# A state-space scan in tiles of four states by thirty-two channels, run on from one sequence into the next

## The reference, cut to what matters

```python
x = x + _layernorm(_L1_attn_ref(_layernorm(x), ...))     # the Mamba layer, third of four blocks
...
delta = jax.nn.softplus(dt_full + b_dt)                  # 512 channels by 512 tokens
def step(state, inp):                                    # over the 512 tokens
    u, dlt, Bs, Cs = inp
    dA = jnp.exp(dlt.reshape(b, NC, DPG)[..., None] * A_g)
    du = (dlt * u).reshape(b, NC, DPG)
    state = dA * state + du[..., None] * Bs[:, :, None, :]
    y = jnp.einsum('bgdn,bgn->bgd', state, Cs).reshape(b, D_INNER)
    return (state, y)
...
y = (ys.transpose(1, 0, 2) + x.transpose(0, 2, 1) * D_param) * jax.nn.silu(z)
return y @ W_out.T
```

## Time and profile before

| what | value |
|---|---|
| median of 3 runs | 2097.48 us |
| the profiled execution's own time | 2099.33 us |
| its span, first to last instruction | 2097.5 us |
| mean granted TensorE clock | 0.899 |
| VectorE (DVE) busy | 1770.0 us, 84% |
| TensorE matmuls (PE) busy | 1651.5 us, 79% |
| ScalarE (ACT) busy | 1035.9 us, 49% |
| GpSimd (POOL) busy | 913.8 us, 44% |
| DMA, share of 16 engines | 23%, 157.95 MB |
| the eight scans, first to last | 231.47 to 2001.45 us |

### The profile page before, as it was taken

One profiled execution on the slowest core, in us unless ns is written; L12 is line 12 of the kernel. 1 busy time (PEld: TensorE's weight loads), 2 busy tenths in 40 slices (PEclk: granted clock), 3 DMA queues, 4 the chain that ended last, 5 costly groups with the idle time before them and its releaser, 6 DMA issues. The chain is left out here.

```text
span 2097.5 us, 22567 instructions
## 1 busy us (share of the span) xinstructions
PE 1651.5 (79%) x5875; PEld 725.3 (35%) x5948; DVE 1770.0 (84%) x3142; ACT 1035.9 (49%) x1745; POOL 913.8 (44%) x676
## 2 busy tenths in 40 slices
PE   3375577778996889868997799878997899779856
PEld 1122123232452335322452335332452335234324
DVE  6577899989879998979989998999989987987830
ACT  3247444825555454735556355734547344734312
POOL 0101534454437434554346434464346544665510
PEclk9977699979997999979997899979997899999978
DMA  4100222222222222222231222222222223223300
GB/s 108 46 0 21 72 79 89 92 69 77 75 92 65 85 71 86 85 67 78 74 101 65 81 76 76 96 75 72 76 96 71 76 85 106 86 99 113 110 10 11
DMA packets 94601, 157.95 MB, mean 75 GB/s; under 512 B 10940, under 2 KB 23660, under 8 KB 94468
## 3 DMA queue, kind: packets, MB, share of 16 engines
q1 hardware_dynamic: 94468, 156.43, 22.9%
HBM read 143.83 MB, written 12.58 MB: 75 GB/s over the span
## 5 line engine op out<-in xcount | busy, mean ns | idle before, releaser
L1226 POOL TENSOR_TENSOR prod<-state,c_all 128x512 f32<-128x512 f32 x512 | 669.6, 1312 | 706.8 <-DVE state L1203 644.0
L1203 DVE TENSOR_TENSOR_SCAN state<-decay,ps_b 128x512 f32<-128x512 f32 x512 | 619.7, 1210 | 9.7 <-issue 0.4
L750 PE MATMUL ps_y<-prod,idf 128*128 128x512 f32 x1024 | 610.6, 689 | 4.8 <-DVE u L1216 3.6
L1210 DVE TENSOR_TENSOR ps_b<-du,ps_b 128x512 f32<-128x512 f32 x512 | 347.7, 679 | 87.3 <-PE ps_b L743 86.8
L919 ACT ACTIVATE decay<-delta,a_neg 128x512 f32<-128x512 f32 x512 | 359.3, 719 | 32.3 <-DVE state L1203 29.3
L743 PE MATMUL ps_b<-b_rows,sel_b 48*128 48x512 bf16 x512 | 209.9, 411 | 155.0 <-DVE state L1203 152.7
L750 PEld LDWEIGHTS ps_y<-prod,idf 128*128 128x128 f32 x1024 | 183.8, 207 | 136.3 <-issue 109.9
L743 PEld LDWEIGHTS ps_b<-b_rows,sel_b 48*128 48x128 bf16 x512 | 47.8, 94 | 467.3 <-DVE state L1203 332.5
L619 PE MATMUL ps_x<-xT,w 128*128 128x512 bf16 (+1 forms) x391 | 132.0, 422 | 80.1 <-DVE arena_l L1095 65.6
L826 ACT ACTIVATE arena_l<-ps_x 128x512 f32<-128x512 f32 (+1 forms) x104 | 61.8, 594 | 190.8 <-PE ps_x L619 189.7
L535 PE MATMUL ps_x<-hT,win 128*128 128x512 bf16 (+1 forms) x455 | 135.6, 441 | 21.4 <-DVE arena_b L1171 16.6
(11 more groups left out here) (230 smaller groups left out, 2422.2 us busy)
## 6 DMA issues: line engine op xcount, KB each, us to landing
c_all<-c_rows SPq DMA_DIRECT2D x512, 256.0 KB
c_rows<-arena_l SPq DMA_DIRECT2D x32, 256.0 KB
out<-arena_b SPq DMA_DIRECT2D x8, 512.0 KB
x_in<-in_base SPq DMA_DIRECT2D x8, 256.0 KB
c_all<-in_winT SPq DMA_DIRECT2D x1, 1280.0 KB, 7.5
arena_b<-in_w_fc SPq DMA_DIRECT2D x1, 1024.0 KB, 5.7
arena_b<-in_w_proj SPq DMA_DIRECT2D x1, 1024.0 KB, 5.0
w<-in_w1T SPq DMA_DIRECT2D x1, 792.0 KB, 5.9
```

Source lines behind the costliest of these rows:

```text
L750: nc.tensor.matmul(ps_y[:], idf[:], prod[:, n % NP, :], start=(n % NST == 0), stop=(n % NST == NST - 1)).then_inc(reduced, 1)
L1203: nc.vector.tensor_tensor_scan(state[:, n % NS, :], decay[:, n % NDA, :], ps_b[:, n % NDB, :], 0.0, ALU.mult, ALU.add).then_inc(scanned, 1)
L1210: nc.vector.tensor_tensor(ps_b[:, j % NDB, :], du[:, slot(s, ct), :], ps_b[:, j % NDB, :], ALU.mult).then_inc(driven, 1)
L1226: nc.gpsimd.tensor_tensor(prod[:, n % NP, :], state[:, n % NS, :], c_all[:, n % NC, :], ALU.mult).then_inc(multiplied, 1)
```

## The change

A tile now has 32 channels with four states each: partition 64g + 16s + c holds channel 16g + c of the 32 and state s of the four. A block of 128 channels still has 16 tiles: n % 4 (called q) says which 32 channels, n % 16 // 4 which four states.

- **Sums.** The selector `sel_y` (128x32) adds the four states of each channel and puts out 32 columns, into partitions 32q to 32q+31 of `ps_y`. The sums of tiles 4m to 4m+3 stand together in part 2 of step 4m+6, behind one wait for all four, with one semaphore update behind the last. So `ps_y` takes four matmuls of 32 columns in place of four of 128, the number of matmuls is the same, and GpSimd's wait for tile n-4 to be summed becomes one for the group.
- **delta and du** are no longer usable as they are computed. `d_store` (two DMAs of 256 KB a block) puts them into DRAM, and `scan_sync` reads them back repeated (for each q, two DMAs of 128 KB for delta and two for du) in the steps 12 to 15 of a block, once the tile in this place is decayed and driven: 16 DMAs a block, 64 a sequence, and 8 stores. SyncE's 64 loads of C stay.
- **Run on.** `tile_at` maps a tile outside 0 to 63 to the neighbouring sequence. The steps are 0 to 63 only; the last tiles of s are scanned, multiplied and summed in the first steps of the iteration of s+1, without empty steps between. LATE is laid into the steps 0 to 60, BACK and GATE into the steps 6 to 63. Within a slot the chains come ahead of the scan.
- The logarithm of softplus now comes after `d_fix`, the storage of its steps is moved, and exp(A_log) is laid out and negated on ScalarE.

```diff
         def scan_pe(...):
+                nc.tensor.matmul(ps_b[:, n % NDB, :], sel_s[lo:lo + 48, part_n, :],
                                  b_rows[lo:lo + 48, s.par, ct // 2, :], start=True, stop=True).then_inc(b_spread, 1)
-            if part == 2:
-                for n in sums_at(j):
-                    if n % NST == 0:
-                        wait(eng, y_taken, s.count(PER, n))
-                    eng.wait_ge(multiplied, s.count(PER, n + 1))
-                    nc.tensor.matmul(ps_y[:], idf[:], prod[:, n % NP, :], start=(n % NST == 0),
-                                     stop=(n % NST == NST - 1)).then_inc(reduced, 1)
+            s, n = tile_at(at, j - 3)
+            if part == 2 and exists(s) and n % QN == QN - 1:
+                ct, part_n, q = parts(n)
+                if part_n == 0:
+                    wait(eng, y_taken, s.count(PER, NST * ct))
+                eng.wait_ge(multiplied, s.count(PER, n + 1))
+                for q in range(QN):
+                    ins = nc.tensor.matmul(ps_y[q * QC:(q + 1) * QC, :], sel_y[:], prod[:, (n - QN + 1 + q) % NP, :],
+                                           start=(part_n == 0), stop=(part_n == QN - 1))
+                ins.then_inc(reduced, QN)
...
         def scan_sync(...):
+            for n in range(-QN, 0) if j == -1 else [j] if j % NST >= NST - QN else []:
+                q = n % QN
+                s, to = tile_at(at, n + QN)
...
+                eng.wait_ge(d_stored[ct], stored)
+                wait(eng, decayed, used)
+                wait(eng, driven, used)
+                for kind, rep in enumerate((delta, du)):
+                    rows = d_rows[s.par, ct, kind].rearrange("(q g o c) t -> q g o c t", q=QN, g=QG, o=1)[q]
+                    for g in range(QG):
+                        eng.dma_start(rep[64 * g:64 * (g + 1), q, :],
+                                      rows[g].broadcast_to([QN, NST, T])).then_inc(d_spread[q], 16)
...
-        SLOTS = [(j, part, 1.0 if 0 <= j <= PER else 0.25) for j in STEPS for part in range(3)]
+        SLOTS = [(j, part) for j in range(PER) for part in range(3)]
+        ALL = [1.0] * len(SLOTS)
+        AHEAD = [1.0 if j < PER - 3 else 0.05 for j, _ in SLOTS]
+        BEHIND = [1.0 if j > Y_LAG else 0.0 for j, _ in SLOTS]
...
-            for k, (j, part, _) in enumerate(SLOTS):
-                fns["scan"](eng, s, j, part)
+            for k, (j, part) in enumerate(SLOTS):
                 for slots in chains:
                     run_steps(e, eng, fns, slots[k])
+                fns["scan"](eng, s, j, part)
```

More of the change, by code:

```diff
@@ L29 @@
 NST = 16
+QN = 4
+QC = P // QN
+QG = QC // NST
 NXB = 4
@@ L335, in sandwich @@
         u = sb("u", [P, 2, CT, T])
-        delta, du = (sb(n, [P, CT + 1, T]) for n in ("delta", "du"))
+        delta, du = (sb(n, [P, QN, T]) for n in ("delta", "du"))
+        d_r = sb("d_r", [P, 2, T])
         NC, NDA, NDB, NS, NP = 5, 4, 2, 3, 4
@@ L436, in sandwich @@
         out_stored = sem("out_stored")
+        d_stored = [sem(f"d_stored{i}") for i in range(CT)]
+        d_spread = [sem(f"d_spread{i}") for i in range(QN)]
         b_spread = sem("b_spread")
@@ L822, in late_act @@
                     wait(eng, late["V"], s.count(LPER, 0))
+                    for k in range(CT):
+                        wait(eng, d_stored[k], s.count(PER, 0))
                 if i >= 2:
@@ L861, in late_act @@
                 eng.wait_ge(late["P"], la(s, "P", ("d", i)))
-                free_slot(eng, s, i)
+                for k in range(2):
+                    if i == 0:
+                        wait(eng, d_stored[k], s.count(PER, 0))
+                    elif i == 2:
+                        eng.wait_ge(c_stored[k], s.count(PER, PER))
                 bank = D_BANK[i]
                 act(d_t(i), ps_x[:, bank, :], ACT.Abs, bias=b2[:, i:i + 1])
-                ins = act(delta[:, slot(s, i), :], ps_x[:, bank, :], ACT.Relu, bias=b2[:, i:i + 1])
+                ins = act(d_raw(i), ps_x[:, bank, :], ACT.Relu, bias=b2[:, i:i + 1])
             elif name == "d_exp":
@@ L1453, in program @@
             together(e, eng, fns, tagged("late", Seq(0), LATE), tagged("early", Seq(1), EARLY), tagged("quant", None, QUANT))
+            for part in range(3):
+                fns["scan"](eng, Seq(0), -1, part)
             iteration(e, eng, fns, Seq(0), first=True)
@@ L1459, in program @@
                 iteration(e, eng, fns, Seq(n))
+            for j in range(PER, PER + Y_LAG):
+                for part in range(3):
+                    fns["scan"](eng, Seq(NBATCH - 1), j, part)
             alone(e, eng, fns, tagged("back", Seq(NBATCH - 1), BACK))
```

203 lines of the change are left out of this document (119 added, 84 removed).

## The result

The changed kernel takes **2591.8 us** (median; the undisturbed runs are 2588.9 to 2593.3, and one of 4202 us is left out as disturbed), the kernel before 2096.4 in the same series: ratio 1.235, 95% interval 1.230 to 1.239. It is 495 us slower, where 2049 us, 2% faster, was forecast. The span is 2591.5 us and the mean granted clock 0.721, against 0.899.

What follows compares the result with a forecast made beforehand. VectorE, 91% full, was taken to set the time. Start 235.5, sequences 219, 1144, 195.6 and 156.8, tail 97.5: 2048.6 us; 2050.4 with 1.8 around the span, less 1.9 for the median: 2049 us, range 1988 to 2115.

Steps and rivals of the forecast that it cites:

- Spreading delta and du, "at nothing": SyncE's stores and repeats at changes of block: issues fit the steps and landings are hidden, so no added time.
- The forecast's slack: Repeats on SyncE: the one for tile n is due four steps, 14 us, after its issue can start.
- The rival of late repeats: SyncE's in-order queue: repeats wait behind loads of C, 1.5 us at each of 31 block changes, 2096 us; chance 0.10.
- theory C: From the experiments, not the prediction: SyncE's order puts repeats behind loads of C; no size at the start.
- The added wait, 3 us a sequence: GpSimd's four product buffers return together, so product and scan wait: 3 us a sequence, 22 in the last.
- S + 2.0 against a room of 5.55: Middle sequences: from scan 4m+5's end, the group's time plus 2.0 us must fit VectorE's 5.55 us of other work.
- The wait for the spread of B, 10.3 becomes 6: VectorE's drive waiting for TensorE's spread: falls with TensorE's load, from 10.3 to 6 us a middle sequence.
- S, 2.5 us: Time of a group of four sums on TensorE: staggered halves in five places, 2.15 us, plus 0.33 for switches.
- side by side in full: Rival for TensorE's four sums: all run at once, a group takes 0.9 to 1.2 us, 1997 us total; chance 0.22.
- the emptying at a switch of shape: TensorE switching to 32 columns and back: at most about 0.17 us each, 0.33 for two.
- The lower clock: Rival for a lighter TensorE: half speed for a third of groups, some 40 us, 2090; within the forecast's range, no separate chance.
- VectorE's busy time: Sign in the profile after: VectorE still busy 217 us a sequence, its instructions unchanged.

Runs made afterwards that it cites:

- e1: The changed kernel with each repeat reading 64 consecutive rows instead of 16 rows four times, giving wrong delta and du: 2311.6 us, ratio 1.103.
- e5: The changed kernel with channels outermost and copies inside, a repeat being one 128-row transfer and a load of C two of 64 rows: 2281.7 us, ratio 1.091.
- e11: e5 with the sums issued in pairs of column groups instead of fours: 2102.8 us, ratio 1.003.
- e13: e5, still with groups of four sums, with six product buffers instead of four and two decay buffers instead of four: 2138.7 us, ratio 1.021.
- e7: e5 with every spread of B issued three times, adding 1024 short matmuls without changing results: 2373.8 us, ratio 1.133.
- e10: The kernel before the change, with only the dealing of both chains over the steps taken from the change: 2173.7 us, ratio 1.037.

## Why the prediction was wrong

**The two causes.** They form a square: fours and copies outermost 2592 (the change), fours and channels outermost 2282, pairs and copies outermost 2429, pairs and channels outermost 2103. The layout is worth 310 with fours and 326 with pairs, the pairs 163 and 179. They add up nearly, and together, 489 us, they are nearly all of the 495. What is left after both, some 6 us, is a balance: the new dealing (77 on the kernel before) and the repeats (16) against what the run-on and the sums side by side win. That balance was not taken apart further, and how much of it is the run-on stays open.

**Spreading delta and du, "at nothing": the step that failed first.** It took the landing time of 128 KB, 2.7 us, from a load of the weights with 128 partitions outermost, for a transfer whose outermost size is 4. The four tiles' repeats move 2 MB; at the 100 GB/s of the trace they need some 20 us by themselves, and with the loads of C on the same engines the tiles came 7 us apart: from the first issue at 931.9 to the fourth tile's decay at 962.6 are 31 us. The forecast's slack was 14 us for the first tile and three steps of 3.4 more for the fourth, 24 in all. The number of issues was right, their length not: 0.51 us alone, but up to 2.98 us while much is queued:

```profile
L1354 SPq DMA_DIRECT2D delta<-d_rows x256: 507/525/2977, 225.5 to 2447.1; - x128
```

The rival of late repeats named the place (the change of block) and priced it at 1.5 us; 310 / 31 is 10. It looked at SyncE's queue, which is theory C, and with all engines at work the repeats as a whole cost 16 us.

**The added wait, 3 us a sequence: the second.** The formula, S + 2.0 against a room of 5.55, was right about who waits for whom, and its S was even too large. What failed is the sentence behind it, "TensorE's own chain work stands ahead of some groups: I put 3 us". In the middle sequences 71 of 80 groups made GpSimd wait, and two things come between a product and its sum. One is the steps' chain matmuls, up to 5.7 us in one piece in e1. The other is TensorE's own wait: the group stands behind a spread of B, and the spread waits for a scan. Spreads did so 116 times in these sequences, for 251 us of idle TensorE, though not all of them ahead of a group. Around the group at 1055.48 this is 6.5 of the 13.7 us that GpSimd stood:

```profile
1054.95 0.60 PE L770 MATMUL ps_b<-b_rows,sel_s 48*128 48x512 bf16 x1 [6.49 <-DVE state L1236]
...
1057.67 1.26 POOL L1260 TENSOR_TENSOR prod<-state,c_all 128x512 f32<-128x512 f32 x1 [13.68 <-PE ps_y L779]
```

Late repeats add to the second, by the scans that they hold up: with channels outermost (e5) GpSimd's wait for the sums is 919 us of 1140. The kernel before hid all this: a buffer came back after each sum, and GpSimd had three more. 179 us over the run, some 22 a sequence, against the 3 (22 in the last) of the forecast. How it divides between the two was not measured.

**The wait for the spread of B, 10.3 becomes 6.** Wrong in its direction: it is 109.5 us in the five middle sequences, 22 each. The sum held that a TensorE with less to do would be less late; in e1's rows the same 5.7 us of chain matmuls hold up the spread.

**S, 2.5 us.** Wrong, and the rival "side by side in full" right: 1.06 us at the high clock. In the changed kernel at the low one:

```profile
1055.48 1.93 PE L779 MATMUL ps_y<-prod,sel_y 128*32 128x512 f32 x8
```

Eight halves in 1.93 us at 1.2 GHz, where the earlier trace rows has four halves in 3.79. The second half of a sum does stand behind its first, as I argued, but the first halves of the other sums do not wait for it. TensorE in e1, in 772.2 to 772.4 and in 772.75 to 773.0:

```profile
772.06 0.64 PE L779 MATMUL ps_y<-prod,sel_y 128*32 128x512 f32 x4
...
772.51 0.61 PE L779 MATMUL ps_y<-prod,sel_y 128*32 128x512 f32 x4
```

The four first halves start within 0.02 us, the four second halves 0.45 us behind them: two places, not five. The other term of S, the emptying at a switch of shape, can be read off too. The next matmul of 128x128 starts 0.43 us behind the start of a sum's last half in the kernel before, and 0.52 behind it in e1 (the fourth of the halves below starts at 847.69). The first two rows are of the kernel before, in 1223.2 to 1223.6, the others of e1, in 848.05 to 848.5:

```profile
1222.92 0.59 PE L750 MATMUL ps_y<-prod,idf 128*128 128x512 f32 x1
1223.35 0.59 PE L722 MATMUL ps_x<-arena_b,fcT 128*128 128x512 f32 x1
...
847.67 0.61 PE L779 MATMUL ps_y<-prod,sel_y 128*32 128x512 f32 x4
848.21 0.70 PE L749 MATMUL ps_x<-arena_b,fcT 128*128 128x512 f32 x1
```

That is 0.1 us a switch at the high clock, where I allowed 0.17. The Trainium skill, "TensorEngine Tiling (Array Packing)", Key Properties, names such an emptying; the trace agrees in that a pause stands there, with this time. But toward a spread of B, 48 rows by 128 columns, the kernel before has it already: 0.53 us from 1961.55, the last half of the sum at 1961.12 in the earlier trace rows, to the spread at 1962.08. That TensorE had less to do did help where single sums became pairs; with groups of four the order took it back, and the rival's 1997 us fails with the forecast's wait.

**The lower clock.** It came, 0.72 for 0.91 in the middle sequences, lower than that rival had it, but nothing here shows it as a large cause of its own: e11 runs at 0.81 and takes what the kernel before takes, e13 takes 143 us less than e5 at the same clock, and more matmuls did not raise it (e7). It lengthens the chain matmuls that stand ahead of a group, which is part of the 179; how much was not separated.

**What held.** VectorE's busy time; the end of the wait for `ps_y` at the ends of a sequence; the tail (97.5 forecast, 96.2); a new wait of the scan for GpSimd, but in all sequences. The gap between the last scan of a sequence and the first of the next did not close: from start to start 5.5 to 7.7 us in six places and 16.8 in one (8.0 to 15.7 before); with channels outermost and pairs (e11) five of the seven are 2.6 to 2.9 us, so there the gap is closed as forecast. The first scan was to come at 235.5 and came at 241.98. The repeats for tiles 0 to 3 and the loads of C behind them were slow there as well:

```profile
225.48 1.44 SPq L1354 DMA_DIRECT2D delta<-d_rows  x2
...
234.57 0.72 ACT L942 ACTIVATE decay<-delta,a_neg 128x512 f32<-128x512 f32 x1 [6.76 <-DMA du<-d_rows]
...
241.98 1.19 DVE L1236 TENSOR_TENSOR_SCAN state<-decay,ps_b 128x512 f32<-128x512 f32 x1
```

**The arithmetic.** The terms of the sum add up to 2048.4 and not 2048.6, and 16 instructions of 256 columns in 3.72 us give 0.44 and not 0.43 us for 512; neither matters.

**What was not in it:** the dealing of the chains. In e10 the sum of the steps' weights falls from 66 to some 61.5 for one chain and 59.8 for the other, which looked like nothing, and costs 77 us.

## What to carry to other kernels

Before a transfer is put down as hidden, price it by a row of its own shape, with the outermost dimension above all: copies outermost cost 310 us more than channels outermost here, and with channels outermost the same bytes cost 16. When work is grouped, count the buffers that come back together against the longest stretch of other work ahead of the group on its engine, not against the group's own time; half the group in the same buffers took 179 us less. A lighter engine helps where others wait for its load, and brings nothing where they wait for its order.

## What the hardware showed that I had not expected

Four fp32 matmuls of 32 columns each (`128*32`, 512 moving columns) in four column groups take 1.06 us together at the high clock and 1.93 at the low one, against an estimated 3.4 at the high clock for four sums of 128 columns, one after another (eight halves of 0.43). A switch between 32 and 128 columns takes some 0.1 us. Transfers of 128 KB with four copies outermost move about 100 GB/s together while several are queued, and stores with eight outermost about 200. And 1024 more short matmuls did not raise the granted clock (0.759 to 0.756).
